# Router logits of a fused decoder layer: gate weights stationary, tokens moving, then turned into rows

## What is computed

```python
def _L0_ffn_ref(x, Wg, W1, b1, W2, b2):
    B, S, H, E, K, F = (4, 512, 256, 8, 128, 1024)
    b, s, h = x.shape
    logits = jnp.einsum('bsh,eh->bse', x, Wg)
    Sm = jnp.swapaxes(jax.nn.softmax(logits, axis=-1), 1, 2)
    G, I = jax.lax.top_k(Sm, K)
    ex = jnp.take_along_axis(x[:, None, :, :], I[..., None], axis=2)
    h1 = jax.nn.gelu(jnp.einsum('bekh,ehf->bekf', ex, W1) + b1[None, :, None, :])
    out = jnp.einsum('bekf,efh->bekh', h1, W2) + b2[None, :, None, :]
    out = G[..., None] * out
    new_x = jnp.zeros_like(x).at[jnp.arange(b)[:, None, None], I].add(out)
    return new_x
```

## Time and profile before

| | us |
|---|---|
| median of 3 runs | 942.67 (942.16 to 943.93) |
| the profiled execution, its own time | 944.04 |
| its span, first to last instruction | 942.3 |
| PE busy | 892.0 (95% of the span) |
| PE weight loads busy | 815.4 (87%) |
| DVE busy | 599.3 (64%) |
| ACT busy | 579.7 (62%) |
| POOL busy | 79.2 (8%) |
| share of PE in the chain that ended last | 85% |

### The profile page before, as it was taken

One profiled execution on the slowest core, in us unless ns is written; L12 is line 12 of the kernel. 1 busy time (PEld: TensorE's weight loads), 2 busy tenths in 40 slices (PEclk: granted clock), 3 DMA queues, 4 the chain that ended last, 5 costly groups with the idle time before them and its releaser, 6 DMA issues.

```text
span 942.3 us, 17858 instructions
## 1 busy us (share of the span) xinstructions
PE 892.0 (95%) x6672; PEld 815.4 (87%) x6672; DVE 599.3 (64%) x1246; ACT 579.7 (62%) x991; POOL 79.2 (8%) x116
## 2 busy tenths in 40 slices
PE   4759888999999999999999999999999999999997
PEld 3659888889988988989998989889998999899997
DVE  5888879777656574665676564656756564433574
ACT  4438875786655666665566666655666665444684
POOL 2330012000110010200120001200110000000000
PEclk8669989999999999999999999999999999999999
DMA  7617999967755554555645454554545455555340
GB/s 226 211 48 247 363 349 314 316 211 247 234 179 151 172 163 144 165 169 156 187 127 177 159 183 153 151 175 156 173 131 184 148 173 167 191 192 164 114 137 12
DMA packets 144693, 172.43 MB, mean 183 GB/s; under 512 B 11208, under 2 KB 110816, under 8 KB 144608
## 3 DMA queue, kind: packets, MB, share of 16 engines
q1 hardware_dynamic: 144608, 171.29, 56.6%
HBM read 135.60 MB, written 35.65 MB: 182 GB/s over the span
## 4 chain that ended last, share of the span: by engine, by line
PE 85%; DVE 8%; ACT 4%; issue 1%; DMA 0%; POOL 0%; SPq 0%; POOLq 0%; ACTq 0%; DVEq 0%
PE down_ps L736 13%; PE down_ps L737 12%; PE down_ps L738 12%; PE up_ps L511 12%; PE up_ps L513 12%; PE up_ps L512 12%; PE bank L564 2%; PE bank L511 2%; PE bank L513 1%; PE bank L512 1%; PE bank L550 1%; PE bank L533 1%; DVE w_lo L893 1%; ACT h_all L836 1%; PE bank L582 1%
## 5 line engine op out<-in xcount | busy, mean ns | idle before, releaser
L836 ACT ACTIVATE h_all<-up_ps,b_all 128x512 f32<-128x512 f32 (+1 forms) x296 | 183.3, 635 | 256.7 <-PE up_ps L513 255.2
L893 DVE TENSOR_TENSOR h_lo<-h_all,h_hi 128x512 fp32r<-128x512 f32 x256 | 177.5, 693 | 221.3 <-ACT h_hi L827 220.8
L736 PE MATMUL down_ps<-w_hi,h_hi 128*128 128x256 f32 x1024 | 295.3, 288 | 2.9 <-DVE acc L1074 2.9
L737 PE MATMUL down_ps<-w_lo,h_hi 128*128 128x256 f32 x1024 | 289.9, 283 | 0.0
L738 PE MATMUL down_ps<-w_hi,h_lo 128*128 128x256 f32 x1024 | 289.6, 283 | 0.0
L511 PE MATMUL up_ps<-x2t_hi,w_hi 128*128 128x512 f32 (+1 forms) x592 | 222.5, 376 | 1.6 <-DVE x2t_lo L893 0.9
L513 PE MATMUL up_ps<-x2t_hi,w_lo 128*128 128x512 f32 (+1 forms) x592 | 217.1, 367 | 0.0
L512 PE MATMUL up_ps<-x2t_lo,w_hi 128*128 128x512 f32 (+1 forms) x592 | 216.3, 365 | 0.0
L736 PEld LDWEIGHTS down_ps<-w_hi,h_hi 128*128 128x128 f32 x1024 | 195.3, 191 | 11.6 <-issue 2.0
L737 PEld LDWEIGHTS down_ps<-w_lo,h_hi 128*128 128x128 f32 x1024 | 196.0, 191 | 6.8
L738 PEld LDWEIGHTS down_ps<-w_hi,h_lo 128*128 128x128 f32 x1024 | 195.8, 191 | 0.0
(11 more groups left out here) (193 smaller groups left out, 997.7 us busy)
## 6 DMA issues: line engine op xcount, KB each, us to landing
w_hi<-w_parts SPq DMA_DIRECT2D x200, 256.0 KB, 3.0
w_lo<-w_parts SPq DMA_DIRECT2D x200, 256.0 KB, 3.3
w_raw<-in_w_dram SPq DMA_DIRECT2D x96, 256.0 KB, 4.0
w_parts<-w_hi SPq DMA_DIRECT2D x64, 256.0 KB, 3.9
w_parts<-w_lo SPq DMA_DIRECT2D x64, 256.0 KB, 4.3
x_in<-in_x_dram SPq DMA_DIRECT2D x8, 256.0 KB, 3.8
ctx_sb<-in_ctx_dram SPq DMA_DIRECT2D x8, 256.0 KB, 3.9
out_dram<-acc SPq DMA_DIRECT2D x8, 256.0 KB, 2.5
```

The source lines that it names most:

```text
L736: nc.tensor.matmul(ps, hi, w2h[:, c, :], start=c == 0 and j == 0, stop=False, skip_group_check=True)
L737: nc.tensor.matmul(ps, hi, w2l[:, c, :], start=False, stop=False, skip_group_check=True)
L836: a = nc.scalar.activation(h_all[:, unit % HALL, k * wide:(k + 1) * wide], up_ps[unit % 2][:, k * wide:(k + 1) * wide], ACT.Gelu_apprx_tan ...
L893: return nc.vector.tensor_tensor(dst, src, hi.bitcast(F32), ALU.subtract)
```

## The change

The logits are computed the other way round. The gate weights (16 or 8 columns) are the stationary side and all 256 tokens of the pair move, which makes 4 matmuls of 8; the logits then lie as 16 rows of 256 tokens. DVE copies them from the bank to a new tile `logits_t`, and PE turns the two halves of it back (2 transposes, 16 rows of 128 columns stationary, 16 columns moving) into the place where the old logits lay. This is a new step, `R_LOGITS_T`, one item after `R_LOGITS`. `R_MAX` moves one item later for pairs 1 to 7. For pair 0, R_MAX and R_GATE leave the order ahead of the expert line and go to items 2 and 3; step T_1 of pair 1 goes from item 1 to item 2, W_1 from 5 to 6. R_GATE of pair 2 goes from item 91 to 92.

```diff
@@ PE, route
-                    for t in range(PAIR):
-                        rows = slice(t * S, (t + 1) * S)
-                        ps = logits_bank(b)[:, t * 2 * E:(t + 1) * 2 * E]
-                        for kc in range(C):
-                            nc.tensor.matmul(ps, x2t_hi[:, kc, b % 3, rows], wg_both[:, kc].rearrange("p k e -> p (k e)"),
-                                             start=kc == 0, stop=False, skip_group_check=True)
-                            mm = nc.tensor.matmul(ps[:, 0:E], x2t_lo[:, kc, b % 3, rows], wg_both[:, kc, 0, :],
-                                                  start=False, stop=kc == C - 1, skip_group_check=True)
+                    ps = logits_bank(b)[0:2 * E, 0:TOK]
+                    for kc in range(C):
+                        nc.tensor.matmul(ps, wg_both[:, kc].rearrange("p k e -> p (k e)"), x2t_hi[:, kc, b % 3, :],
+                                         start=kc == 0, stop=False, skip_group_check=True)
+                        mm = nc.tensor.matmul(ps[0:E], wg_both[:, kc, 0, :], x2t_lo[:, kc, b % 3, :],
+                                              start=False, stop=kc == C - 1, skip_group_check=True)
+                    mm.then_inc(logits_t_ps, 1)
+                if part == 6:
+                    pe.wait_ge(logits_t_ready, b + 1)
+                    for t in range(PAIR):
+                        mm = nc.tensor.transpose(logits_bank(b)[:, t * 2 * E:(t + 1) * 2 * E], logits_t[:, t * S:(t + 1) * S],
+                                                 ident[0:2 * E, 0:2 * E])
                     mm.then_inc(logits_ps, 1)
@@ DVE, route
+                if part == 1:
+                    dve.wait_ge(logits_t_ps, b + 1)
+                    nc.vector.tensor_copy(logits_t[:], logits_bank(b)[0:2 * E, 0:TOK]).then_inc(logits_t_ready, 1)
@@ tables
-          BACK: -9, NORM2: -7, R_TURN: -5, R_LOGITS: -3, R_MAX: -2, R_GATE: 0, R_GATE_T: 3, R_BIAS: 5}
+          BACK: -9, NORM2: -7, R_TURN: -5, R_LOGITS: -3, R_LOGITS_T: -2, R_MAX: -1, R_GATE: 0, R_GATE_T: 3, R_BIAS: 5}
...
-                  (1, E_0), (1, E_1), (0, R_MAX), (0, R_GATE)])
-FIRST_ROUTE = {0: [1], 6: [4], 8: [5]}
+                  (1, E_0), (1, E_1)])
+FIRST_ROUTE = {0: [1], 1: [6], 2: [2], 3: [3], 6: [4], 8: [5]}
```

More of the change, by code:

```diff
@@ L201, in decoder_layer @@
         x2t_lo = sb("x2t_lo", [P, C, 3, TOK], F32R)
+        logits_t = sb("logits_t", [2 * E, TOK])
         logits = sb("logits", [P, PAIR, E])
@@ L333, in decoder_layer @@
         x2t_ready = sem("x2t_ready")
+        logits_t_ps = sem("logits_t_ps")
+        logits_t_ready = sem("logits_t_ready")
         logits_ps = sem("logits_ps")
@@ L1236 @@
  ATT, CTX, WO, NORM1, Y1, XEXP, REC_0, REC_1, REC_2, REC_3, BACK, NORM2,
- R_TURN, R_LOGITS, R_MAX, R_GATE, R_GATE_T, R_BIAS) = range(51)
+ R_TURN, R_LOGITS, R_MAX, R_GATE, R_GATE_T, R_BIAS, R_LOGITS_T) = range(52)
 DIAGONAL = (DIAG_0, DIAG_1)
@@ L1241 @@
 RECUR = (REC_0, REC_1, REC_2, REC_3)
-ROUTE = (R_TURN, R_LOGITS, R_MAX, R_GATE, R_GATE_T, R_BIAS)
+ROUTE = (R_TURN, R_LOGITS, R_MAX, R_GATE, R_GATE_T, R_BIAS, R_LOGITS_T)
 JOIN = (0, 5, 9, 13, 17, 21, 25, 29)
@@ L1248 @@
           ATT: -24, CTX: -23, WO: -21, NORM1: -19, Y1: -18, XEXP: -18, REC_0: -18, REC_1: -16, REC_2: -14, REC_3: -13,
-          BACK: -9, NORM2: -7, R_TURN: -5, R_LOGITS: -3, R_MAX: -2, R_GATE: 0, R_GATE_T: 3, R_BIAS: 5}
+          BACK: -9, NORM2: -7, R_TURN: -5, R_LOGITS: -3, R_LOGITS_T: -2, R_MAX: -1, R_GATE: 0, R_GATE_T: 3, R_BIAS: 5}
 EARLY = [
-    {T_0: 1, T_1: 1, W_0: 4, W_1: 5, S_2: 8, M_2: 8, S_3: 8, M_3: 8, E_2: 11, E_3: 11, T_2: 14, T_3: 15, W_2: 17, W_3: 18, ATT: 20, CTX: 20,
+    {T_0: 1, T_1: 2, W_0: 4, W_1: 6, S_2: 8, M_2: 8, S_3: 8, M_3: 8, E_2: 11, E_3: 11, T_2: 14, T_3: 15, W_2: 17, W_3: 18, ATT: 20, CTX: 20,
      WO: 22, NORM1: 24, Y1: 26, XEXP: 26, REC_0: 26, REC_1: 27, REC_2: 28, REC_3: 28, BACK: 31, NORM2: 31, R_TURN: 33,
-     R_LOGITS: 35, R_MAX: 36, R_GATE: 41, R_GATE_T: 50, R_BIAS: 51},
+     R_LOGITS: 35, R_LOGITS_T: 36, R_MAX: 37, R_GATE: 41, R_GATE_T: 50, R_BIAS: 51},
     {X: 26, X_LOW: 27, X_BIAS: 27, QK: 29, K_COPY: 29, Q_COPY: 29, K_LOW: 30, DIAG_0: 32, Q_LOW: 32, V: 32, V_ADD: 34, V_SPLIT: 35,
@@ L1256 @@
      T_2: 60, T_3: 61, W_2: 64, W_3: 65, ATT: 68, CTX: 69, WO: 71, NORM1: 73, Y1: 76, XEXP: 76, REC_0: 76, REC_1: 77, REC_2: 79,
-     REC_3: 80, BACK: 84, NORM2: 85, R_TURN: 87, R_LOGITS: 89, R_MAX: 90, R_GATE: 91, R_GATE_T: 95, R_BIAS: 97}]
+     REC_3: 80, BACK: 84, NORM2: 85, R_TURN: 87, R_LOGITS: 89, R_LOGITS_T: 90, R_MAX: 91, R_GATE: 92, R_GATE_T: 95, R_BIAS: 97}]
 LAG = 3
```

## The result

The changed kernel took **951.22 us** (median of 5, 949.88 to 951.65), the kernel before 942.67: a ratio of 1.0086, 95% interval [1.0075, 1.0097], or +8.1 us [7.1, 9.1]. The prediction was 946.4 us with a range up to 949.3. The direction was right, the size was not: the time lies above the range. The profiled execution took 951.6 us, its span is 949.9.

The account below looks back on a forecast made before the run. PE was taken to bound the kernel from 200 to 800 us, with PE, ACT and DVE taking turns earlier. 0.3 + 1.5 + 1.55 + 0.4 = 3.75 us on 942.67 gave 946.4 us, range 943.5 to 949.3.

Parts of the forecast that it names:

- half clock: Rival, chance 0.22: PE's clock falls after pair 0's new idle, T_1 and the up behind take 1.4 us more, 947.8 us.
- PE where it is full: Late pairs, logits and transposes on PE: 0.93 us against 0.89, +0.04 us a pair, +0.3 us for 7 pairs.
- the bias matmuls: Late pairs: two neighbours with 24 rows, 128 columns stationary, taking 0.62 us; the basis for 0.45 us for the transposes.
- the lower bound: Late pairs: the new transposes as cheap as the gate transposes, 0.23 us; as rival "cheap transposes" 944.8 us, chance 0.12.
- Pair 0, time of the wait: PE, T_1 of pair 1: waits for DVE's R_MAX, which PE sees at about 76.9 us.
- Pair 0, length of the wait: PE ahead of T_1: a new idle of 2.1 to 2.6 us, to 76.9.
- Pair 0, cost of the wait: PE, item 4: starts at about 79.2 to 79.3 in place of 77.77 us, +1.5 us.
- Pair 0, loads of tables: ACT, around 80 to 84 us: two more loads, 2.6 us, covered by its idle time; cost nothing, up to 0.8.
- Sum for pair 0: Pair 0 (items 0 to 3): +1.5 us from T_1's wait, nothing for the loads of tables or the earlier logits.
- Pair 1, wait: PE, scores of pair 2: start 1.55 us later (1.4 to 1.9), behind the copy and one more w_lo and h_lo.
- Pair 2: R_GATE at item 92, ACT's table load behind a Gelu, ahead of the xt_lo that PE awaits: +0.4 us, 0 to 0.8.
- Absorbed waits: Rival, chance 0.16: PE's wait at 108.6 to 110.2 and later ones give back half or more of 3 us, 943.9 us.

Follow-up runs that it names:

- e5: The changed kernel with matmuls of no use (24 and 20) on PE just ahead of its two waits for R_MAX: 947.33 us, 1.0048 of the kernel before.
- e10: The changed kernel with a plain copy for the exponential of pair 0's routing on ACT, without the two loads of tables: 1.0062 of the kernel before.
- e9: The changed kernel with POOL's four steps on v_cat for pair 2 waiting for the first step of pair 1's R_MAX: 1.0063 of the kernel before.

## Why the prediction was wrong, step by step

The step that failed is the clock. The sum took full speed behind both lengthened waits: for pair 0 half clock stood beside it as a rival at 0.22, for pair 1 nowhere. The runs showed 1.6 and 1.5 us of it (e5), 3.1 of the 3.4 us that the sum lacks in the trace (7.1 for 3.75). The other misses nearly cancel.

- **PE where it is full.** Forecast +0.04 us a pair, measured -0.02 by the rows of the last pair and -0.07 by the shifts; the rest of the difference stays unexplained. Logits 0.45 for 0.48, transposes 0.42 for 0.45: the bias matmuls were the right neighbour, and the lower bound (0.23) fell. Two loads of 16 rows by 128 columns cost 0.42 us with 16 columns moving; two of the old logits' loads, 128 rows by 128 columns, 0.22. The Trainium skill (TensorE: Matmul & The Clock Gate, LDWEIGHTS) states that the time of a load goes by its columns and that rows don't matter. The loads' own rows don't speak against it (0.13 and 0.14 us for the two of 16 rows, 0.19 for those of 128), but the time that the pair takes in the stream doesn't follow from it, and why it doesn't is open.
- **Pair 0, time of the wait.** Right: 76.9 forecast, 77.41 seen with 0.44 us of late start.
- **Pair 0, length of the wait.** 3.12 us for 2.1 to 2.6, since the clock had come up earlier and PE was done earlier. This alone costs nothing.
- **Pair 0, cost of the wait.** Right: +1.5 forecast for item 4, 1.54 measured once the clock stays up (e5).
- **Pair 0, clock.** The failed choice: a rival at 0.22, though its price (1.4 us) was near the 1.6 that e5 shows at item 4. My argument against it was one wait of 2.07 us without a fall.
- **Pair 0, loads of tables.** "Cover is enough, by 0.6 us" failed. Forecast 0 (to 0.8), measured 0.7 (e10). I had summed ACT's idle time; the queue that waited was DVE's, and from 84 to 100 us it had no slack left (15.35 of 16 us).
- **Sum for pair 0**: forecast 1.5; measured 3.8 = 1.5 wait + 1.6 clock + 0.7 behind item 4.
- **Pair 1, wait.** Forecast 1.55, measured 2.1. The copy was right (0.35 taken; the next step starts 0.33 us after it). The extra w_lo and h_lo were priced at 0.60 each from rows where POOL was already done; the moved step stands where POOL works, as these rows of the trace of before show, which I had not used, though the prediction speaks of such a stretch at pair 2:

```profile
152.39 1.59 DVE L893 TENSOR_TENSOR w_lo<-w_raw,w_hi 128x512 fp32r<-128x512 f32 x1
153.91 1.11 DVE L893 TENSOR_TENSOR h_lo<-h_all,h_hi 128x512 fp32r<-128x512 f32 x1
```

e9 shows the cause.

- **Pair 1, clock.** Not in the sum at all: I had no rival for it, and it cost 1.5 us (e5).
- **Pair 2.** Forecast +0.4, measured 0.
- **Absorbed waits** (0.16): not seen; PE's later waits kept their length (1.84 and 3.89 us for 1.81 and 3.88).

In us by the trace: +3.8 (pair 0) + 3.6 (pair 1) - 0.3 (late pairs) = 7.1, and 0.44 at the start.

## What to carry to other kernels

A wait that is lengthened on a full engine costs more than its length: where its clock can fall behind it, price the work behind the wait at half speed too, and do so at every wait that grows. A step moved in one engine's queue takes the price of the place that it is moved to: look at which other engine is busy there, and look for the cover in the queue that will wait, not in the one that does the step. When two traces are compared, read the shift on the engine that bounds the kernel: a shift on another one (here DVE, 4.3 for 3.8 us) may still be made up. And before a new formulation is blamed or praised, run the old one at the new places.
